# Two top-2 mixture stages: normalisation one beat earlier, sums moved between turns, gate write moved to SyncE

## The reference

```python
def _L1_ffn_ref(x, router_w, router_b, expert_w, expert_b):
    router_probs = softmax(x @ router_w + router_b, axis=-1)
    top_p, top_i = top_k(router_probs, 2)
    top_p = top_p / sum(top_p, axis=-1, keepdims=True)
    expert_out = einsum('bnd,edc->bnec', x, expert_w) + expert_b
    gathered = take_along_axis(expert_out, top_i[..., None], axis=2)
    return einsum('bnk,bnkc->bnc', top_p, gathered)

t = t + _L1_ffn_ref(layer_norm(t), ...)      # t: 4 x 16384 tokens of 64 channels
```

## Time and profile before

| | us |
|---|---|
| median of 3 executions | 6381.72 |
| lowest and highest | 6374.5, 6381.86 |
| the profiled execution | 6386.21 |
| span of its trace | 6384.4 |
| first mixture, of the span | about 1795 to 2470 |
| second mixture, of the span | about 5600 to 6384 |

### The profile page before, as it was taken

One profiled execution on the slowest core, in us unless ns is written; L12 is line 12 of the kernel. 1 busy time (PEld: TensorE's weight loads), 2 busy tenths in 40 slices (PEclk: granted clock), 3 DMA queues, 4 the chain that ended last, 5 costly groups with the idle time before them and its releaser, 6 DMA issues. The chain is left out here.

```text
span 6384.4 us, 130690 instructions
## 1 busy us (share of the span) xinstructions
PE 5113.4 (80%) x47166; PEld 3326.0 (52%) x47166; DVE 4324.8 (68%) x9480; ACT 3445.5 (54%) x6809; POOL 1147.4 (18%) x1068
## 2 busy tenths in 40 slices
PE   7887886449958885799969998308999999858887
PEld 4665663224523332699969994104555555523332
DVE  7896887696657777622223447697777777668886
ACT  5664665475545554522243225366767777645554
POOL 2332332162200002400000000131112222221110
PEclk9998998759979997699989999659999999979998
DMA  1111113232348885200000124237666666547776
GB/s 36 35 31 35 38 35 90 62 105 85 109 165 267 269 271 164 74 0 0 0 0 0 66 101 132 66 99 94 81 81 81 81 81 83 65 159 231 234 231 214
DMA packets 745076, 646.31 MB, mean 101 GB/s; under 512 B 496551, under 2 KB 578663, under 8 KB 744627
## 3 DMA queue, kind: packets, MB, share of 16 engines
q1 hardware_dynamic: 734387, 634.86, 40.2%
q10 hardware_dynamic: 9216, 4.20, 0.2%
q0 software_dynamic: 1024, 1.05, 0.1%
HBM read 549.78 MB, written 90.20 MB: 100 GB/s over the span
## 5 line engine op out<-in xcount | busy, mean ns | idle before, releaser
L2424 PE MATMUL sw_pC<-sw_row,sw_wc 128*128 128x128 f32 x10160 | 1159.8, 275 | 56.2 <-DVE sw_row L2299 54.9
L2424 PEld LDWEIGHTS sw_pC<-sw_row,sw_wc 128*128 128x128 f32 x10160 | 1148.6, 191 | 58.3 <-DVE sw_row L2299 55.5
L2858 PE MATMUL sp_pC<-sp_work,sp_bands 64*64 64x512 f32 (+11 forms) x14592 | 985.5, 428 | 43.4 <-issue 43.4
L2287 DVE SCALAR_TENSOR_TENSOR sw_row<-sw_pC,sw_y 128x128 f32<-128x128 f32 x1016 | 337.5, 332 | 793.0 <-PE sw_pC L2424 793.0
L2858 PEld LDWEIGHTS sp_pC<-sp_work,sp_bands 64*64 64x64 f32 x14592 | 600.3, 133 | 431.8 <-issue 363.8
L2797 ACT ACTIVATE sp_pC<-sp_pC,sp_par 128x512 f32<-128x512 f32 x832 | 598.5, 741 | 369.8 <-PE sp_pC L2858 346.7
L1823 DVE TENSOR_TENSOR t_z<-t_z,t_ht 128x1024 f32<-128x1024 f32 x512 | 619.1, 1244 | 107.7 <-DMA t_z<-gate_rows 105.4
L2356 ACT ACTIVATE sw_y<-sw_row 128x128 f32 (+1 forms) x762 | 265.2, 348 | 593.8 <-DVE sw_row L2287 593.8
L2001 PE MATMUL t_pO<-t_z,t_ew 128*64 128x512 f32 x2048 | 511.0, 626 | 35.7 <-DVE t_z L1823 34.5
L2754 DVE TENSOR_TENSOR sp_work<-sp_work,sp_pC 128x512 f32<-128x512 f32 x512 | 351.1, 687 | 169.0 <-ACT sp_pC L2797 168.5
L1969 PE MATMUL t_pT<-t_ident,t_h 128*128 128x128 f32 x1024 | 162.5, 311 | 293.3 <-ACT t_ht L1881 169.7
(11 more groups left out here) (385 smaller groups left out, 9663.3 us busy)
## 6 DMA issues: line engine op xcount, KB each, us to landing
t_z<-gate_rows SPq DMA_DIRECT2D x512, 512.0 KB, 7.4
sp_bands<-windows SPq DMA_DIRECT2D x128, 512.0 KB
c_spent<-tokens SPq DMA_DIRECT2D x128, 256.0 KB, 2.7
cb_xs<-tokens SPq DMA_DIRECT2D x128, 256.0 KB, 2.8
wa_xs<-in_x SPq DMA_DIRECT2D x64, 256.0 KB, 3.0
tokens<-wa_xt SPq DMA_DIRECT2D x128, 128.0 KB, 1.9
tokens<-cb_h SPq DMA_DIRECT2D x64, 256.0 KB, 2.7
t_xs<-tokens SPq DMA_DIRECT2D x32, 512.0 KB, 9.5
```

The source lines that it names most:

```text
L2287: dve.scalar_tensor_tensor(row[par][c][:, :, PAD:PAD + P2], pC[c][:, 0:2 * P2].rearrange("p (b w) -> p b w", b=2), 0.0, line(sweep, c, i), ...
L2424: ins = pe.matmul(pC[c][:, 0:2 * P2], wc[:, sweep, m, :], row[1 - par][c][:, :, m:m + P2], start=(m == 0), stop=(m == 4))
L2858: ins = pe.matmul(out[halves[to], :, low * lo:low * hi], band[halves[k], (NV * g + j) % BANDS, q, AT[k][tap], :], v[halves[k], :, low * at ...
```

## The change

- TensorE: `add_rest` of the last beat's second half and of this beat's first half stand between and behind the two turns. `mix(n, 1)` is split: its first pair goes between `logits` and `turn_logits`, the other three behind. The last `add_rest` stands behind the loop.
- ScalarE: `normalise` works on m+1 = n+3 instead of m, and stands behind `save_logits`; the beat begins with `save_gates`. The DMA that writes the gates, and its wait, are gone from ScalarE. `save_mixed(n, 1)` is last, and `finish(n, 1)` is done in the next beat. The prologue also normalises beat 2.
- VectorE: in the second mixture `stats` and `norm` work on n+4; those of beat 3 are in the prologue, `stats` ahead of `route(1)`.
- SyncE: `keep_gates` waits for the copied gates and issues their write; it stands just ahead of `spread_gates(n+1, 0)`. In the second mixture the loads of columns run two tiles further ahead: the prologue loads tiles 7 to 10, where it loaded 7 and 8.

```diff
+            def keep_gates(m):
+                sp.wait_ge(gs_saved, m + 1)
+                sp.dma_start(gate_rows[m, :, :].rearrange("e (j p) -> (e j) p", p=128),
+                             gs[:, m % 2, :]).then_inc(g_out[m % 2], 16)
...
+            keep_gates(0)
             for i in range(2):
                 spread_gates(0, i)
                 if rows is not None:
-                    load_columns(7 + i)
+                    load_columns(7 + 2 * i)
+                    load_columns(8 + 2 * i)
             for n in range(NB):
-                if rows is not None and 2 * n + 9 < 2 * NB:
-                    load_columns(2 * n + 9)
+                if rows is not None and 2 * n + 11 < 2 * NB:
+                    load_columns(2 * n + 11)
                 if n + 1 < NB:
+                    keep_gates(n + 1)
                     spread_gates(n + 1, 0)
...
-                if rows is not None and 2 * n + 10 < 2 * NB:
-                    load_columns(2 * n + 10)
+                if rows is not None and 2 * n + 12 < 2 * NB:
+                    load_columns(2 * n + 12)
...
@@ VectorE, beat and prologue
-                if carried is None and n.plus(3).within(NB):
-                    stats(n.plus(3))
+                if carried is None and n.plus(4).within(NB):
+                    stats(n.plus(4))
...
-                if carried is None and n.plus(3).within(NB):
-                    norm(n.plus(3))
+                if carried is None and n.plus(4).within(NB):
+                    norm(n.plus(4))
...
             gate(first)
+            if carried is None:
+                stats(first.plus(3))
             route(first.plus(1))
+            if carried is None:
+                norm(first.plus(3))
@@ ScalarE, save_gates and beat
-                act.wait_ge(gs_saved, m.n + 1)
-                act.dma_start(gate_rows.rearrange("m e t -> m (e t)")[bass.ds(m.n, 1), :].rearrange(
-                    "a (k p) -> (a k) p", p=128), gs[:, m.k % 2, :]).then_inc(g_out[m.k % 2], 16)
...
                 due = m.within(NB)
-                if due:
-                    normalise(m, 0)
+                ahead = m.plus(1)
                 if n.plus(1).within(NB):
                     save_gates(n.plus(1))
                 if due:
-                    normalise(m, 1)
                     save_turned(m, 0)
                 save_mixed(n, 0)
+                if n.n > 0:
+                    finish(n.plus(-1), 1)
                 if due:
                     save_turned(m, 1)
+                finish(n, 0)
+                if due:
                     for i in range(2):
                         save_logits(m, i)
-                if carried is None and n.plus(3).within(NB):
-                    root(n.plus(3))
-                save_mixed(n, 1)
-                finish(n, 0)
+                if ahead.within(NB):
+                    normalise(ahead, 0)
+                if carried is None and ahead.plus(1).within(NB):
+                    root(ahead.plus(1))
+                if ahead.within(NB):
+                    normalise(ahead, 1)
                 if due:
                     gap(m)
-                finish(n, 1)
+                save_mixed(n, 1)
@@ TensorE, beat
-                mix(n, 0, n.plus(1) if n.plus(1).within(NB) else None)
+                mix(n, 0, range(4), n.plus(1) if n.plus(1).within(NB) else None)
+                if due:
+                    turn(m, 0)
+                if n.n > 0:
+                    add_rest(n.plus(-1), 1)
+                if due:
+                    turn(m, 1)
+                add_rest(n, 0)
                 if due:
                     for i in range(2):
-                        turn(m, i)
-                    route(m)
-                mix(n, 1)
-                for i in range(2):
-                    add_rest(n, i)
+                        logits(m, i)
+                mix(n, 1, [0])
+                if due:
+                    for i in range(2):
+                        turn_logits(m, i)
+                mix(n, 1, [1, 2, 3])
```

More of the change, by code:

```diff
@@ L1953, in _ @@
             prepare(first.plus(1), first)
+            for i in range(2):
+                normalise(first.plus(2), i)
             gap(first.plus(1))
+            if carried is None:
+                root(first.plus(3))
             over_beats(act, beat)
+            finish(Beat(NB - 1, (NB - 1) % 6, (NB - 1) // 6), 1)
         @block.tensor
@@ L1992, in turn_gates, with mix @@
                              ident[:, :]).then_inc(gates_turned, 1)
-            def mix(m, i, gates_of=None):
+            def mix(m, i, pairs, gates_of=None):
                 since(pe, oc_saved, 2 * m.n + i - 1)
-                for q in range(4):
+                for q in pairs:
                     if gates_of and q == 2:
@@ L2012, in add_rest @@
                 ins.then_inc(out_ready, 1)
-            def route(m):
-                for i in range(2):
-                    logits(m, i)
-                for i in range(2):
-                    turn_logits(m, i)
             def prepare(m, gates_of=None):
@@ L2042, in _ @@
             over_beats(pe, beat)
+            add_rest(Beat(NB - 1, (NB - 1) % 6, (NB - 1) // 6), 1)
 def stage_sweeps(nc, tok, kernels):
```

## The result

The changed kernel takes 6397.07 us, the median of 11 executions (6389.79 to 6402.76), beside 6380.24 us for 11 of the kernel before on the same chip: a ratio of 1.0026, with a 95% interval of 1.0017 to 1.0034. It is slower by 17 us. The profiled execution took 6400.48 us, with a span of 6398.7 us, 14.3 more than before.

What follows compares the result with a forecast made beforehand. Each beat was taken as a chain of waits, held after the change by a loop over VectorE and TensorE. Terms +4 + 0 + 13 - 4.5 = +12.5, rounded to +13, gave 6395 us on the median's scale; range 6330 to 6440.

Steps and rivals of the forecast that it cites:

- The removed wait: TensorE's 3.05 us wait at each beat's second turn goes; at most 95 us per mixture could be had.
- The loop of the first mixture, 19.6 us: Chain over VectorE (10.0 us) and TensorE (9.6 us, sums and first mix pair included) sets the first mixture's beat.
- The rival by which little comes in the wait's place: Both mixtures: the wait goes, beats fall to 18.9 and 21.0 us, total 6338 us; chance 0.28.
- The clock, 0.25 us a beat: TensorE's clock falls less often, partly where it waits for VectorE; cost 0.25 us per beat, between 0 and 1.0.
- The rival of a clock lost in TensorE's half: Clock falls in TensorE's half of the loop; beats cost 1.0 us over full clock, total 6437 us; chance 0.17.
- "I take nothing" for the queue: Gates' write on SyncE's queue behind `z` loads: cost between -2 and +5 us, taken as nothing because the path has slack.
- The rival with a chance of 0.15 and 18 us: The queue bounds the first mixture: write behind loads adds 0.6 us a beat, 18 us, total 6408 to 6413; chance 0.15.
- my signs: Trace checks listed beforehand: wait gone, TensorE idling 2 to 3 us, score waits near 4.5 and 3, gate spacings, later start.
- The second mixture's beat, 21.95: Second mixture: loop 21.3 plus clock 0.25 plus GpSimd 0.4 gives 21.95 us a beat, equal to before.
- The start, +13: Second mixture's start: `stats(3)` ahead of `route(1)` waits for tile 7, delaying beat 1's first product; +13 us, +10 to +18.
- Ends, -4.5: Ends of both mixtures: one `add_rest` less behind the last mix, -1.85 and -2.7 us, together -4.5.
- ScalarE "isn't on the loop, so nothing": On ScalarE, the gates' write issue and wait, some 0.6 us, go; taken as worth nothing.

Runs made afterwards that it cites:

- e1: The changed kernel with the write of the gates issued by ScalarE again, right behind the copy: 6386.29 us, ratio 1.0009.
- e6: The changed kernel with SyncE's load of later tokens issued between the write of the gates and the wait for it: 6378.02 us, ratio 0.9995.
- e2: The changed kernel with the first pair of `mix(n, 1)` behind `turn_logits` again: 6384.46 us, ratio 1.0006.
- e3: The changed kernel with `add_rest(n, 0)` behind the last mix pair and `finish(n, 0)` last on ScalarE: 6350.78 us, ratio 0.9962.
- e4: The changed kernel with both sums and the first mix pair behind `turn_logits`, as before; `normalise` stays a beat ahead: 6334.04 us, ratio 0.9931.
- e7: The changed kernel with the second mixture's statistics three beats ahead, `norm` ahead of `route`, and column loads as before the change: 6379.16 us, ratio 0.9999.
- e8: The kernel before, with only the write of the gates moved from ScalarE to SyncE: 6349.81 us, ratio 0.9958.
- e5: The changed kernel with both sums and the first pair behind, as before, and the gates' write on ScalarE: 6289.37 us, ratio 0.9859.
- e9: The changed kernel with both sums and the pair behind, the gates' write on ScalarE, and second-mixture statistics three beats ahead: 6281.69 us, ratio 0.9852.

## Why the prediction was right, and where it wasn't

The forecast was 6395 us and slower; measured were 6397.07 us and slower by 0.26%, with an interval of 0.17 to 0.34% that reaches under the 0.2% which I had called the bound. That the sum comes out within 2 us is luck. In the first mixture two errors of 25 and 16 us go against each other and leave 9 us too much in the forecast; in the second three errors leave 13 too little.

| term | forecast | measured |
|---|---|---|
| first mixture, its loop and end | +4 - 1.85 | -22.8 (e1's length less that of before): beats -18.8, end -4.5, start +0.6 |
| first mixture, the queue | 0 | +15.7 (after less e1) |
| second mixture, start | +13 | +15.7 |
| second mixture, its beats | 0 | +7.2 (from beat 1 to the last beat's first product) |
| second mixture, end | -2.7 | +0.7 |
| stages untouched | 0 | -2.3 |

- **The removed wait**: right. It isn't in the list of after, and the most that it could bring wasn't had. In its place TensorE waits for the products, 2.59 us in the beat shown above, as forecast.
- **The loop of the first mixture, 19.6 us**: right as a mechanism, 0.7 us too long. Bare, in e1 and e6, it is 18.9 to 19.0. VectorE's half is 9.8 us: from the second score copy at 2106.15 to 2110.06, and to 2115.94. TensorE's is 18.9 - 9.8 = 9.1 and not 9.6; measured in e1 from the end of the fourth product to the end of `turn_logits` it is 9.2 (median). From start to start in the timeline of after, a turn takes 2120.61 - 2119.73 = 0.88 us where I had 0.99, the sum ahead of it 2119.73 - 2117.98 = 1.75 where I had 1.85, and the two `logits` together 1.0 where I had 1.28. The rival by which little comes in the wait's place had 18.9 for this beat, and so the better number here.
- **The clock, 0.25 us a beat**: too much for the first mixture. In e1, 13 beats of it have no stretch at 0.50 and take 18.9 us, and 16 have one and take 19.1: the stretch costs 0.2 in every second beat, since it falls on the part that VectorE's products pace. In the kernel before it fell on turns and sums, in 22 of 29 beats, and these took 19.9 us where the seven at full clock took 19.1. So most of the 18.8 us that the beats of e1 gained is clock given back: 22 x 0.8 = 18 less 16 x 0.2 = 3 makes 15, an estimate. I had the 0.8 and credited the change with too little of it. The rival of a clock lost in TensorE's half is refuted: in the changed kernel 2 beats of 29 in each mixture have any of it on turns, sums or scores.
- **"I take nothing" for the queue**: this is the step that failed. The rival with a chance of 0.15 and 18 us was the right one for the first mixture: 15.7 us by the profiled lengths, 10.8 by the medians. My reason was a slack of several us on the path from the gates to `z`, and I had reckoned it for one beat. But the queue has a period of its own: its bytes, and the 2 us that it stands empty from the write's landing to the first bytes of the loads that waited for it. That gap stood in the kernel before already, and I didn't price it. Once the loop was down to 18.9, the queue's period of some 19.6 was the longer one: the changed kernel keeps the loop's pace for ten beats, until the slack is used up. Of my signs, the copied gates 19.64 us apart fell into the range of 19.5 to 20.2, but it was the queue that set them, and the scores' wait was 12.1 / 21 = 0.6 us a beat where I had 4.5. By my own list, I was wrong if the `z` loads ended most of VectorE's idle time, and they do: 87.1 us. That sign was a poor one, since it held in the kernel before too.
- **The second mixture's beat, 21.95**: 22.1 from product to product, where before had 21.7 (medians), and I had equality. The scores' wait is 69.6 / 25 = 2.8 us each time, near the 3 forecast. The loop is what holds it: e2, e3 and e4 shorten it one after the other. Its parts are close to what I had: TensorE's half 11.1 us (median) for 11.3. VectorE's is 4.9 and 5.8, together 10.7, for 10.4 with GpSimd's 0.4. GpSimd's sum meets the routing there: one comparison takes 1.62 us beside it and 0.29 otherwise, in the timeline of a beat at 5957. The clock is the term that was too small: leaving out the storing beats and others over 24 us, those with one stretch at 0.50 take 21.9 us on average, those with two 22.7, and the one without 20.7. These stretches take 92 us of 5700 to 6190 where they took 75 before. That they lengthen the beat, and not the other way round, wasn't tried.
- **The start, +13**: its mechanism is as forecast: the first product 17.6 us later, where 17.3 was worked out, and beat 1 15.7 later, inside the 10 to 18. e7 takes 14.6 of them back.
- **Ends, -4.5**: in the first mixture the stage from the last beat's first product is 5.5 us shorter (27.6 to 22.1); in the second it isn't (33.3 to 34.0). I had named `add_rest` as the last thing ahead of the stores there, and why it isn't wasn't tried.
- **ScalarE "isn't on the loop, so nothing"**: right for the changed kernel, where e1 and e6 have the same first mixture with and without its issue. In the kernel before, e8 shows the move to be worth 30 us. The change took this gain and most of the wait's away from itself by putting the sums in their place.

**What stays open.** In e4 the loop no longer holds the second mixture: the scores end only 4.4 us of VectorE's idle time from 5700 to 6330 us, and the loads 39.8. VectorE waits for nothing else there that the profile lists, and is busy 540 of the 630 us, so VectorE itself, with its loads, is the likely next limit; it wasn't tried. How much of the 65 us is the clock's isn't known. Nor is it known why the landing in the kernel before is tied to the last load although the write has a queue of its own. e2 has 6 us more than the changed kernel in the first mixture; its profiled execution is itself 4.8 us above its median.

## What to carry to other kernels

Before a term is set to nothing because its path has slack, ask for the whole period of the resource. A queue whose issuer waits for a write and then issues what depends on it has a period of its own: the time for its bytes plus the time that it is empty. An independent load in that gap (e6) or a queue of its own for the small write (e1) was worth 15 us of 673 here, and 47 once the loop was out of the way (e5). And when work is moved to fill one engine's wait, look where the next loop closes. Work between an engine's last input and what the other engine waits for is paid in every beat, less what the engine would have waited anyway (1.9 of 2.7 us in e3). The same work behind it wasn't seen to cost anything (e4).

## What was unexpected of the hardware

- A small write on the queue that also has the 512 KB loads lands in 9.0 us, on the other queue of the same engines in 6.2 (e1), and in 1.9 where the loads had nearly drained before it (e6). In the kernel before it is 5.0 and, with the queue alone changed, 9.3 (e8).
- DMA share: 0.83 (270 GB/s) looked like a full transport, but 0.90 (295 GB/s) is had by closing about half of a gap of 2 us in a beat (e4 and e5). The time that `z` needs for its bytes wasn't measured by itself.
- The clock follows the order of the work more than its amount: 0.94 mean over 1860 to 2400 us in the changed kernel, 0.97 with the sums behind, 0.99 in e5, and 1.00 in e9, with more matmuls in the same time.
- What a stretch at 0.50 costs depends on the work that it falls on: 0.8 us of the beat on turns and sums (before), 0.2 on matmuls that wait for VectorE's products (e1).
